# Two fused adjacency layers on one core: the two halves of 20 slots become a ring of 41 slots

## The chip, the cores and the metric

The kernel runs on one core of one Trainium2 chip. The metric is the device time in microseconds (us) of one execution; lower is better. The kernel before took 395.99 us, the median of three runs (395.52 to 396.37).

## The reference, cut to what matters

`x` is 5120 x 64, `adj` is 5120 x 5120, all in f32. The first layer scales and projects the rows of `x` into `e`, multiplies by the adjacency's transpose and by the adjacency, normalises, and adds. The second layer keeps edges only where a softmax passes a threshold; for these inputs none survives, so its message is zero and what is left of it is a second normalisation.

```python
e = concatenate([u, i])                  # rows of x, scaled and projected
h = adj @ (adj.T @ e)
out = layernorm(h) * gamma + beta + x
x1 = _layernorm(x + out)
return _layernorm(x1 + relu(message(x1, adj)))   # message is 0 unless an edge survives
```

An edge can survive only where entries of `adj` are large enough, so the kernel finds the largest sum of squares of a row piece of `adj` and enters the long branch only if it reaches a limit. In these runs it does not.

## The kernel before, in words

**Work and tiling.** `adj` is read from memory once, as ten column blocks of 512 columns (`NB = 10`), and each block as 20 units (`UPB`) of two row tiles: a unit is 128 partitions x 1024 f32, 512 KB, one DMA (line 1033). There are 200 units, numbered `v` through all blocks. One buffer, `pooled`, holds `SLOTS` slots of one unit each, and behind them `h_sum` (128 x 5120), the sum of `h` (lines 103 to 106). Even blocks lie in slots 20 to 39 and odd blocks in slots 0 to 19 (`SLOT_FIRST`, line 44), so the unit that lay in a slot before unit `v` is `v - 40`, the same place two blocks earlier.

**What each unit goes through.** TensorE multiplies it into the block's column sums, `adj.T @ e` (`multiply_unit`, line 1471, 8 records a unit). ScalarE reads it for the sum of squares (`scan`, line 1153): an ACTIVATE that writes a throw-away result into `scratch` (two buffers by turns) and an ACTIVATION_READ_ACCUMULATOR that brings the sum; `scan(v)` waits for `scan(v - 2)`, which used the same scratch buffer. VectorE then turns it in place, 32 x 32 squares at a time (`turn_unit`, line 1265), after both TensorE and ScalarE are through with it.

**What each block goes through.** When the 20 units of block `c` are multiplied, VectorE turns the block's column sums out of PSUM (`turn_half`, line 1274), and ScalarE and GpSimd copy them, 8 copies each in two steps of 4, into `col_sum` (`keep_cols`, lines 1162 and 1084; ScalarE does its part in its own order, after the last scan of the block and before the first of the next). Then TensorE multiplies the turned units by the column sums (`multiply_round`, line 1491, 128 records a round): a round takes some tiles of one block, by `PARTS` (0 to 9, 10 to 23 and 24 to 39 in blocks 0 to 8). VectorE adds each round's PSUM sums to `h_sum` (`add_round`, line 1285, for block 0 a copy, line 1283). A round needs its units turned, `col_sum` kept (first half from the start, second half for its second half of matmuls), and the earlier sums in its PSUM banks added.

**The order of the work** is written out by hand, one list per engine. TensorE in the steady part, for `c` from 1: products of units 0 to 15 of block `c + 1`, first round of block `c`, products of units 16 to 19 of block `c + 1`, second and third round of block `c`. This is called a cycle here; cycle `c` begins with the first product of block `c + 1`. At the start the order is: products of block 0, products of units 20 and 21, first round of block 0 (called R0). VectorE in a cycle: 13 turns, add the first round, a turn, `turn_half`, 5 turns, add the second round, a turn, add the third round. SyncE issues the loads in order of `v`; before loading into a slot it waits until the round that holds the slot's old unit is done (`round_done`, line 1032), and everything after it in SyncE's queue waits too.

**Set-up and end.** `x_first`, `xt_pairs` and small inputs lie in slots 0 to 5 until `e` is made; SyncE waits for that before unit 20 (line 1028). `center_t` and `center_g` are small tiles, written at the start and after R0 (lines 1073, 1250) and read by one small matmul in block 1 (line 1539), whose end is `gamma_turned`. At the end `x` is loaded again (lines 1038 to 1040) into the first slots of block 8 (`X_SLOT`), and seven groups of tiles are normalised and stored while the last four rounds run.

Of the kernel before, what the change touches and what calls it, by code (L numbers as in the profile page):

```python
# [7 lines left out]
def adjacency_layers_kernel(nc, x, adj, w_ui, scales, gamma, beta,  # L8
# [7 lines left out]
    bf16 = mybir.dt.bfloat16  # L16
    i32 = mybir.dt.int32
    ALU = mybir.AluOpType
    ACT = mybir.ActivationFunctionType
    X = mybir.AxisListType.X  # L20

    P = 128
    N, D = x.shape
# [11 lines left out]
    NB = len(WIDTHS)  # L35
# [4 lines left out]
    UNIT_FIRST = [sum(UPB[:c]) for c in range(NB + 1)]  # L40
    UNITS = UNIT_FIRST[NB]

    SLOTS = 40
    SLOT_FIRST = [20 if c % 2 == 0 else 0 for c in range(NB)]
    assert sum(WIDTHS) == N and max(WIDTHS) == CH

    PARTS = [((0, 10), (10, 14), (24, 16))] * (NB - 1)
    PARTS += [((0, 12), (12, 12), (24, 8), (32, 8))]


    ORDER = [(c,) + part for c in range(NB - 1) for part in PARTS[c]]
# [44 lines left out]
    with ctx:  # L96
        def sb(name, shape, dt=f32):
            return ctx.enter_context(nc.sbuf_tensor(name, shape, dt))
# [22 lines left out]
        SETUP_SLOTS = -(-setup_at[0] // SLOT)  # L121


        X_SLOT = 20
        x_at = SLOT * X_SLOT
        x_all = pooled[:, x_at:x_at + T * D].rearrange("p (t d) -> p t d", d=D)
        x_sum, var, rstd, y_var, y_eps, x1_rstd, scale = (
# [15 lines left out]
        rows_in = sb("rows_in", [P, T, D])  # L143
        col_sum = [sb(f"col_sum{k}", [P, CH // 32, D]) for k in range(2)]
        col_half = sb("col_half", [P, CH // 2])
        scratch = [sb(f"scratch{k}", [P, SLOT], bf16) for k in range(2)]
        ident = sb("ident", [P, P])
        center = sb("center", [P, 2 * D])
        gamma_sb = sb("gamma_sb", [D, 1])
        center_t = sb("center_t", [D, P])  # L150
        center_g = sb("center_g", [D, D])
        beta_sb = sb("beta_sb", [P, D])
        beta_sum = sb("beta_sum", [P, 1])
        square_sum = sb("square_sum", [P, UNITS])
# [3 lines left out]
        minus_half = sb("minus_half", [P, GT])  # L158


        piece_at = [N * i for i in range(4)] + [ln_at + N * i for i in range(4)]
        piece = [pooled[:, a:a + N] for a in piece_at]
        assert 4 * N <= x_at and piece_at[-1] + N <= POOLED
        ring, turned, carved_from, rest = piece[0:4], piece[4:6], piece[6], piece[7]
        cols = rest[:, 0:BLOCKS * D].rearrange("p (b d) -> p b d", d=D)
        sums = [rest[:, BLOCKS * D + GROUP * s:BLOCKS * D + GROUP * s + GROUP] for s in range(2)]
# [183 lines left out]

        def slot_of(v):
            c, i = place_of_unit(v)
            return SLOT_FIRST[c] + i

        def before_in_slot(v):

# [55 lines left out]
        def turned_of(g):  # L412

            c, first, nt = place_of_round(g)
            w = WIDTHS[c]
            at = SLOT * SLOT_FIRST[c] + w * first
            return pooled[:, at:at + w * nt].rearrange("p (t b r) -> p t b r", b=w // 32, t=nt)

        def spread_from(c, h, f):
# [596 lines left out]
        @block.sync  # L1016
        def _(sp):
            for k in range(LGROUPS):
                sp.dma_start(x_first[:, group_tiles(k), :], tile_rows(x, GT * k, GT)).then_inc(x_loaded[k], 16)
            for v in range(UNITS):  # L1020
                c, i = place_of_unit(v)
                ut, c0 = UNIT_TILES[c], COL_FIRST[c]
                if v == UNIT_FIRST[1]:
                    sp.dma_start(gamma_sb[:, :], gamma).then_inc(norm_in, 16)
                    sp.dma_start(beta_sb[:, :], beta.partition_broadcast(P)).then_inc(norm_in, 16)

                    assert SLOT_FIRST[1] == 0 and SETUP_SLOTS <= UPB[1]
                    sp.wait_ge(e_made, LGROUPS)
                before = before_in_slot(v)
                if before:  # L1030
                    b, ib = place_of_unit(before[-1])
                    sp.wait_ge(round_done, rounds_through(b, UNIT_TILES[b] * ib))
                sp.dma_start(slots[slot_of(v)].rearrange("p (t k) -> p t k", t=ut),  # L1033
                             tile_rows(adj, ut * i, ut)[:, :, c0:c0 + WIDTHS[c]]).then_inc(unit_loaded[slot_of(v)], 16)


            assert SLOT_FIRST[NB - 2] == X_SLOT and SLOT_FIRST[NB - 1] != X_SLOT
            sp.wait_ge(round_done, ROUNDS_AT[NB - 2] + 1)
            for a, b in ((0, USER_TILES), (USER_TILES, T)):
                sp.dma_start(x_all[:, a:b, :], tile_rows(x, a, b - a)).then_inc(x_again, 16)  # L1040

            survives = edges_may_survive(sp)

            def store_made(k):
                made, by = (out_made_act, BY_ACT) if k in BY_ACT else (out_made, BY_DVE)
                sp.wait_ge(made, by.index(k) + 1)
                store_out(sp, k)

            for k in (0, 1, 2, 4, 5, 3, 6):
                store_made(k)  # L1050
            for k in range(4):
                sp.wait_ge(out_stored[k], 16 * len(range(k, NORMS, 4)))
            with sp.If(survives > 0):
                message_sp(sp)
# [85 lines left out]
        @block.scalar  # L1140
        def _(act):
            act.dma_start(w_ui_sb[:, :], w_ui).then_inc(weights_in, 16)
            act.dma_start(scales_sb[:, :], scales).then_inc(scales_in, 16)

            def copy_pairs(k):
                act.wait_ge(pairs_turned, k + 1)
                act.copy(xt_pairs[:, CH * k:CH * k + CH], pair_bank(k)).then_inc(pairs_copied, 1)  # L1147

            def scan(v):
                wait_loaded(act, v)  # L1150
                if v >= 2:
                    act.wait_ge(unit_scanned, v - 1)
                nc.scalar.activation(scratch[v % 2][:, :], slots[slot_of(v)], ACT.Square,  # L1153
                                     accum_out=square_sum[:, v:v + 1]).then_inc(unit_scanned, 1)

            def keep_cols(c):
                act.wait_ge(halves_turned_b, c + 1)
                if c >= 2:
                    act.wait_ge(round_done, ROUNDS_AT[c - 1])
                for h in range(2):  # L1160
                    for a in range(QUADS):
                        kept = act.copy(spread_to(c, a, h, 0), spread_from(c, h, 0))  # L1162
                    kept.then_inc(cols_kept_act, 1)

            for k in range(LGROUPS - 1):
                copy_pairs(k)
            scan(0)
            copy_pairs(LGROUPS - 1)
            for v in range(1, UNITS):
                c, i = place_of_unit(v)  # L1170
                scan(v)
                if i == UPB[c] - 1:
                    keep_cols(c)
                if c == 1 and i == 16:
                    act.wait_ge(gamma_turned, 1)
                    act.copy(center[:, D:2 * D], bank[3][:, 0:D]).then_inc(center_kept, 1)

            def square_c(k):

                act.wait_ge(nat_made, k + 1)  # L1180
                if k >= 2:
                    act.wait_ge(var_made, k - 1)
                nc.scalar.activation(c_sq[k % 2][:, 0:norm_size(k), 0:D], nat_of(k)[:, 0:norm_size(k), 0:D],  # L1183
                                     ACT.Square, scale=D ** -0.5).then_inc(c_squared, 1)

            def square_y(k):

                act.wait_ge(y_made, k + 1)
                if k >= 2:
                    act.wait_ge(y_var_made, k - 1)  # L1190
                nc.scalar.activation(y_sq[k % 2][:, 0:norm_size(k), 0:D], x_all[:, norm_tiles(k), :],  # L1191
                                     ACT.Square, scale=((1.0 + LN_EPS) / D) ** 0.5).then_inc(y_squared, 1)

            def make_out(k):
                act.wait_ge(scale_made, k + 1)
                for i in range(norm_size(k)):
                    t = norm_tiles(k).start + i
                    made = nc.scalar.activation(ln_o[k % 4][:, i, :], x_all[:, t, :], ACT.Copy, scale=scale[:, t:t + 1])
                made.then_inc(out_made_act, 1)

            square_c(0)
            square_y(0)
            survives = edges_may_survive(act)
            square_c(1)
            square_c(2)
            square_y(1)
            square_y(2)
            square_c(3)
            square_c(4)
            make_out(1)  # L1210
            square_y(3)
            make_out(2)
            square_c(5)
            square_c(6)
            square_y(4)
            square_y(5)
            square_y(6)
            make_out(3)
            with act.If(survives > 0):
                message_act(act)  # L1220

        @block.vector
        def _(dve):
# [35 lines left out]
            def turn_unit(v):  # L1259

                c, i = place_of_unit(v)
                dve.wait_ge(unit_used, v + 1)
                dve.wait_ge(unit_scanned, v + 1)
                tiles = slots[slot_of(v)].rearrange("p (t b r) -> p t b r", t=UNIT_TILES[c], r=32)
                nc.vector.transpose(tiles, tiles).then_inc(unit_turned, 1)  # L1265
# [21 lines left out]
            def add_round(g):  # L1287
                add_tiles(g, *place_of_round(g)[1:])
# [25 lines left out]
            turn_half(1)  # L1314
            for v in range(UNIT_FIRST[1] + 16, UNIT_FIRST[2]):
                turn_unit(v)
            add_round(2)


# [288 lines left out]
```

## Time and profile before

| what | value |
|---|---|
| median of three runs | 395.99 us (395.52 to 396.37) |
| the profiled execution's own time | 397.39 us |
| its span, first to last instruction | 395.5 us |
| TensorE busy | 379.0 us, 96% |
| VectorE busy | 316.7 us, 80% |
| ScalarE busy | 269.1 us, 68% |
| DMA engines, share of the span on the queue of the loads | 76.3% |
| granted TensorE clock, mean | 0.992 |

The span is 1.9 us shorter than the profiled execution's own time, and that time is 1.4 us above the median of the runs. PE is TensorE, PEld its weight loads, DVE VectorE, ACT ScalarE, POOL GpSimd, SP SyncE. Matmul ends in the records are modelled, so starts are the safer numbers: the distance between two starts is what a piece of work takes on TensorE.

### The profile page before, as it was taken

What the parts mean: (1) busy time and instruction counts of PE and PEld (TensorE: products, weight loads), DVE (VectorE), ACT (ScalarE), POOL (GpSimd) and SP (SyncE); (2) the same over time, 40 slices, a digit from 0 to 9 for tenths busy, and PEclk for the clock granted to TensorE, in tenths of its full rate; (3) what the DMA queues carried; (4) which work ended last, traced back from release to release, by engine and by line L of the source; (5) the groups of instructions that cost most, each with busy time, mean ns of one, the idle gap of its engine ahead of it and who ended that gap; (6) DMA issues with size and microseconds to landing.
All of it is one profiled execution on the core that took longest, in us unless ns stands there. A gap on an engine that the chain in (4) does not pass through costs nothing.

```text
span 395.5 us, 13309 instructions
## 1 busy us (share of the span) xinstructions
PE 379.0 (96%) x5762; PEld 220.2 (56%) x5762; DVE 316.7 (80%) x305; ACT 269.1 (68%) x519; POOL 63.8 (16%) x122
## 2 busy tenths in 40 slices
PE   8987999999999999999999999999999999999990
PEld 7743655565465546545654664565466456555770
DVE  1699989797697869687976989697698869795674
ACT  3598996994868658597856868685876778511143
POOL 2001101102100300030030003003000300277375
PEclk9999999999999999999999999999999999999996
DMA  8999999995797799579877958996795799400012
GB/s 291 387 388 382 386 386 384 386 352 192 232 380 267 268 320 391 180 275 389 314 263 272 386 195 277 388 351 230 278 386 191 272 392 383 145 3 2 24 35 85
DMA packets 56991, 109.83 MB, mean 278 GB/s; under 512 B 3808, under 2 KB 4576, under 8 KB 56928
## 3 DMA queue, kind: packets, MB, share of 16 engines
q1 hardware_dynamic: 56640, 108.84, 76.3%
q8 instruction: 47, 0.77, 0.8%
q14 instruction: 16, 0.13, 0.1%
q10 hardware_dynamic: 288, 0.09, 0.1%
HBM read 107.60 MB, written 1.31 MB: 275 GB/s over the span
## 4 chain that ended last, share of the span: by engine, by line
PE 84%; DMA 6%; issue 3%; DVE 3%; POOL 1%; ACT 1%; SPq 1%; POOLq 0%; DVEq 0%
PE quad L1491 45%; PE quad L1471 34%; DMA pooled<-in_adj 6%; PE quad L1506 2%; DVE pooled L1265 2%; PE quad L1513 1%; PE quad L1442 1%; ACT scratch L1153 1%; SPq L1033 1%; PE quad L1452 1%; DVE pooled L1285 1%; POOL pooled L1112 1%; POOL col_sum L1084 0%; POOLq L96 0%; POOL pooled L1107 0%
## 5 line engine op out<-in xcount | busy, mean ns | idle before, releaser
L1153 ACT ACTIVATE scratch<-pooled 128x1024 bf16<-128x1024 f32 x200 | 210.1, 1051 | 39.8 <-DMA pooled<-in_adj 38.0
L1265 DVE STREAM_TRANSPOSE pooled<-pooled 128x1024 f32<-128x1024 f32 x200 | 229.7, 1209 | 3.3 <-ACT scratch L1153 3.2
L1471 PE MATMUL quad<-pooled,rows_in 128*64 128x256 f32 x1600 | 180.2, 381 | 4.3 <-DMA pooled<-in_adj 4.3
L1491 PE MATMUL quad<-pooled,col_sum 32*64 32x320 f32 (+4 forms) x3968 | 177.5, 507 | 0.4 <-POOL col_sum L1084 0.2
L1471 PEld LDWEIGHTS quad<-pooled,rows_in 128*64 128x64 f32 x1600 | 111.9, 137 | 74.3 <-issue 13.1
L1491 PEld LDWEIGHTS quad<-pooled,col_sum 32*64 32x64 f32 x3968 | 87.5, 132 | 83.1 <-issue 64.6
L1285 DVE TENSOR_TENSOR pooled<-pooled,quad 128x1280 f32<-128x1280 f32 (+5 forms) x29 | 52.4, 1808 | 43.8 <-PE quad L1491 43.7
L1084 POOL COPY col_sum<-col_half 32x256 f32<-32x256 f32 x80 | 31.6, 394 | 312.1 <-DVE col_half L1274 309.0
L1162 ACT COPY col_sum<-col_half 32x256 f32<-32x256 f32 x80 | 32.2, 402 | 38.0 <-DVE col_half L1274 37.0
L1153 ACT ACTIVATION_READ_ACCUMULATOR scratch<-pooled 128x1 f32 x200 | 37.4, 187 | 0.0
L1183 ACT ACTIVATE pooled<-quad 128x256 f32<-128x256 f32 (+2 forms) x7 | 3.3, 475 | 23.4 <-PE quad L1506 23.4
L1506 PEld LDWEIGHTS quad<-center,pooled 128*128 128x128 f32 x80 | 9.3, 191 | 3.3 <-issue 1.8
L1506 PE MATMUL quad<-center,pooled 128*128 128x128 f32 x80 | 10.3, 281 | 0.9 <-DVE pooled L1285 0.8
L1274 DVE STREAM_TRANSPOSE col_half<-quad 128x256 f32<-128x256 f32 x10 | 4.5, 445 | 7.2 <-PE quad L1471 7.2
L1112 POOL TENSOR_TENSOR pooled<-pooled,minus_half 128x4 f32<-128x4 f32 (+2 forms) x7 | 8.9, 1276 | 6.5 <-DVE pooled L1369 6.4
L1107 POOL TENSOR_TENSOR pooled<-pooled,minus_half 128x4 f32<-128x4 f32 (+2 forms) x7 | 8.9, 1281 | 5.0 <-DVE pooled L1337 4.8
L1191 ACT ACTIVATE pooled<-pooled 128x256 f32<-128x256 f32 (+2 forms) x7 | 3.6, 507 | 9.1 <-DVE pooled L1364 7.2
L1147 ACT COPY pooled<-quad 128x512 f32<-128x512 f32 x5 | 2.9, 585 | 9.7 <-PE quad L1442 9.7
L1283 DVE COPY pooled<-quad 128x1280 f32<-128x1280 f32 (+2 forms) x3 | 5.8, 1936 | 4.1 <-PE quad L1491 4.1
L1238 DVE TENSOR_TENSOR rows_in<-quad,pooled 128x256 f32<-128x256 f32 x10 | 3.7, 410 | 3.6 <-PE quad L1452 3.3
L1102 POOL TENSOR_TENSOR pooled<-pooled,beta_sb 128x512 f32<-128x512 f32 x5 | 6.4, 1276 | 0.4
L1337 DVE TENSOR_REDUCE pooled<-pooled 128x4 f32<-128x260 f32 (+2 forms) x7 | 3.8, 538 | 2.7 <-ACT pooled L1183 2.7
(45 smaller groups left out, 62.8 us busy)
## 6 DMA issues: line engine op xcount, KB each, us to landing
pooled<-in_adj SPq DMA_DIRECT2D x200, 512.0 KB, 9.4
pooled<-in_x SPq DMA_DIRECT2D x5, 256.0 KB, 3.7
pooled<-in_x SPq DMA_DIRECT2D x1, 768.0 KB, 5.3
pooled<-in_x SPq DMA_DIRECT2D x1, 512.0 KB, 3.8
out<-pooled SPq DMA_DIRECT2D x2, 256.0 KB, 2.5
out<-pooled SPq DMA_DIRECT2D x2, 192.0 KB, 2.4
out<-pooled SPq DMA_DIRECT2D x3, 128.0 KB, 2.1
pooled<-in_w_ui ACTq DMA_DIRECT2D x1, 64.0 KB, 3.3
```

The source lines that it names most:

```text
L1084: kept = nc.gpsimd.tensor_copy(spread_to(c, a, h, 1), spread_from(c, h, 1))
L1102: nc.gpsimd.tensor_tensor(xk, xk, beta_sb[:, :].unsqueeze(1).to_broadcast([P, GT, D]), ALU.add).then_inc(x_steps, 1)
L1107: nc.gpsimd.tensor_tensor(rstd[:, norm_tiles(k)], var[:, norm_tiles(k)], minus_half[:, 0:norm_size(k)], ALU.pow).then_inc(rstd_made, 1)
L1112: nc.gpsimd.tensor_tensor(scale[:, norm_tiles(k)], y_var[:, norm_tiles(k)], minus_half[:, 0:norm_size(k)], ALU.pow).then_inc(scale_made, 1)
L1153: nc.scalar.activation(scratch[v % 2][:, :], slots[slot_of(v)], ACT.Square, accum_out=square_sum[:, v:v + 1]).then_inc(unit_scanned, 1)
L1162: kept = act.copy(spread_to(c, a, h, 0), spread_from(c, h, 0))
L1265: nc.vector.transpose(tiles, tiles).then_inc(unit_turned, 1)
L1283: nc.vector.tensor_copy(to, share).then_inc(round_added, 1)
L1285: nc.vector.tensor_tensor(to, to, share, ALU.add).then_inc(round_added, 1)
L1471: mm = pe.matmul(block_bank(c)[half(h), 0:w // 2], rows_in[:, t, :], slots[slot_of(v)][:, at:at + w // 2], start=(t == 0), stop=(t == T - 1))
L1491: mm = pe.matmul(round_banks(g)[a][half(b % 2), 0:w].rearrange("p (t r) -> p t r", r=32), col_sum[c % 2][quadrant(a), b, :], to[quadrant(a ...
L1506: mm = pe.matmul(nat_of(k)[:, i, :], h_sum[:, P * (first + i):P * (first + i) + P], center[:, :], start=True, stop=True)
```

## The change

The ring has 41 slots, and unit `v` lies in slot `(9 + v) % 41`, so the unit before it in its slot is `v - 41`. A round's turned data must lie in one piece, so in odd blocks a part now ends where the ring wraps round: block 3 has rounds of 10, 16 and 14 tiles, block 5 of 12, 16 and 12, block 7 of 14, 16 and 10; block 1 and the even blocks keep 10, 14 and 16, and block 9 its own four. The order of products and rounds on TensorE is the same, and so are the lists of the other engines. The space for the new slot (4 KB a partition) comes from `scratch`, which is one buffer in place of two, so that `scan(v)` waits for `scan(v - 1)`, and from `center_t` and `center_g`, which now lie in the end of `h_sum`; the third `add_round` therefore waits for `gamma_turned`. SyncE's wait for `e` stands before unit 32 in place of unit 20. `x` is loaded again into slot 5 in place of slot 20, again the first slots of block 8. The pieces of the long branch, which is not entered, are placed elsewhere.

```diff
--- before.py
+++ after.py
@@ -40,12 +40,17 @@
     UNIT_FIRST = [sum(UPB[:c]) for c in range(NB + 1)]
     UNITS = UNIT_FIRST[NB]
 
-    SLOTS = 40
-    SLOT_FIRST = [20 if c % 2 == 0 else 0 for c in range(NB)]
+    SLOTS = 41
+    SLOT_FIRST = [(9 + UNIT_FIRST[c]) % SLOTS for c in range(NB)]
     assert sum(WIDTHS) == N and max(WIDTHS) == CH
 
     PARTS = [((0, 10), (10, 14), (24, 16))] * (NB - 1)
+    PARTS[3] = ((0, 10), (10, 16), (26, 14))
+    PARTS[5] = ((0, 12), (12, 16), (28, 12))
+    PARTS[7] = ((0, 14), (14, 16), (30, 10))
     PARTS += [((0, 12), (12, 12), (24, 8), (32, 8))]
+    assert all((SLOT_FIRST[c] + t // UNIT_TILES[c]) % SLOTS + nt // UNIT_TILES[c] <= SLOTS
+               for c in range(NB) for t, nt in PARTS[c])
 
 
     ORDER = [(c,) + part for c in range(NB - 1) for part in PARTS[c]]
@@ -121,7 +126,7 @@
         SETUP_SLOTS = -(-setup_at[0] // SLOT)
 
 
-        X_SLOT = 20
+        X_SLOT = 5
         x_at = SLOT * X_SLOT
         x_all = pooled[:, x_at:x_at + T * D].rearrange("p (t d) -> p t d", d=D)
         x_sum, var, rstd, y_var, y_eps, x1_rstd, scale = (
@@ -143,12 +148,13 @@
         rows_in = sb("rows_in", [P, T, D])
         col_sum = [sb(f"col_sum{k}", [P, CH // 32, D]) for k in range(2)]
         col_half = sb("col_half", [P, CH // 2])
-        scratch = [sb(f"scratch{k}", [P, SLOT], bf16) for k in range(2)]
+        scratch = sb("scratch", [P, SLOT], bf16)
         ident = sb("ident", [P, P])
         center = sb("center", [P, 2 * D])
         gamma_sb = sb("gamma_sb", [D, 1])
-        center_t = sb("center_t", [D, P])
-        center_g = sb("center_g", [D, D])
+
+        center_t = h_sum[0:D, N - P:N]
+        center_g = h_sum[0:D, N - P - D:N - P]
         beta_sb = sb("beta_sb", [P, D])
         beta_sum = sb("beta_sum", [P, 1])
         square_sum = sb("square_sum", [P, UNITS])
@@ -158,9 +164,9 @@
         minus_half = sb("minus_half", [P, GT])
 
 
-        piece_at = [N * i for i in range(4)] + [ln_at + N * i for i in range(4)]
+        piece_at = [0] + [ln_at + N * i for i in range(7)]
         piece = [pooled[:, a:a + N] for a in piece_at]
-        assert 4 * N <= x_at and piece_at[-1] + N <= POOLED
+        assert N <= x_at and piece_at[-1] + N <= POOLED
         ring, turned, carved_from, rest = piece[0:4], piece[4:6], piece[6], piece[7]
         cols = rest[:, 0:BLOCKS * D].rearrange("p (b d) -> p b d", d=D)
         sums = [rest[:, BLOCKS * D + GROUP * s:BLOCKS * D + GROUP * s + GROUP] for s in range(2)]
@@ -350,7 +356,7 @@
 
         def slot_of(v):
             c, i = place_of_unit(v)
-            return SLOT_FIRST[c] + i
+            return (SLOT_FIRST[c] + i) % SLOTS
 
         def before_in_slot(v):
 
@@ -413,7 +419,7 @@
 
             c, first, nt = place_of_round(g)
             w = WIDTHS[c]
-            at = SLOT * SLOT_FIRST[c] + w * first
+            at = SLOT * slot_of(UNIT_FIRST[c] + first // UNIT_TILES[c])
             return pooled[:, at:at + w * nt].rearrange("p (t b r) -> p t b r", b=w // 32, t=nt)
 
         def spread_from(c, h, f):
@@ -1023,8 +1029,9 @@
                 if v == UNIT_FIRST[1]:
                     sp.dma_start(gamma_sb[:, :], gamma).then_inc(norm_in, 16)
                     sp.dma_start(beta_sb[:, :], beta.partition_broadcast(P)).then_inc(norm_in, 16)
-
-                    assert SLOT_FIRST[1] == 0 and SETUP_SLOTS <= UPB[1]
+                if v < UNIT_FIRST[2] and slot_of(v) == 0:
+
+                    assert c == 1 and i + SETUP_SLOTS <= UPB[1]
                     sp.wait_ge(e_made, LGROUPS)
                 before = before_in_slot(v)
                 if before:
@@ -1148,9 +1155,9 @@
 
             def scan(v):
                 wait_loaded(act, v)
-                if v >= 2:
-                    act.wait_ge(unit_scanned, v - 1)
-                nc.scalar.activation(scratch[v % 2][:, :], slots[slot_of(v)], ACT.Square,
+                if v:
+                    act.wait_ge(unit_scanned, v)
+                nc.scalar.activation(scratch[:, :], slots[slot_of(v)], ACT.Square,
                                      accum_out=square_sum[:, v:v + 1]).then_inc(unit_scanned, 1)
 
             def keep_cols(c):
@@ -1314,6 +1321,7 @@
             turn_half(1)
             for v in range(UNIT_FIRST[1] + 16, UNIT_FIRST[2]):
                 turn_unit(v)
+            dve.wait_ge(gamma_turned, 1)
             add_round(2)
 
 
```

## Rows read from the trace of the kernel before

**Rows 1.** The page: the engines, and the queue of the loads.

```profile
PE 379.0 (96%) x5762; PEld 220.2 (56%) x5762; DVE 316.7 (80%) x305; ACT 269.1 (68%) x519; POOL 63.8 (16%) x122
...
q1 hardware_dynamic: 56640, 108.84, 76.3%
```

**Rows 2.** Timeline of TensorE: cycle 1, and starts in the next three.

```profile
73.86 14.03 PE L1471 MATMUL quad<-pooled,rows_in 128*64 128x256 f32 x128
87.82 4.56 PE L1491 MATMUL quad<-pooled,col_sum 32*64 32x320 f32 x128
92.31 3.67 PE L1471 MATMUL quad<-pooled,rows_in 128*64 128x256 f32 x32
95.92 13.14 PE L1491 MATMUL quad<-pooled,col_sum 32*64 32x448 f32 x256
108.98 13.17 PE L1471 MATMUL quad<-pooled,rows_in 128*64 128x256 f32 x120
...
144.60 12.31 PE L1471 MATMUL quad<-pooled,rows_in 128*64 128x256 f32 x112
...
158.45 1.08 PE L1471 MATMUL quad<-pooled,rows_in 128*64 128x256 f32 x8 [0.29 <-DMA pooled<-in_adj]
...
180.63 9.72 PE L1471 MATMUL quad<-pooled,rows_in 128*64 128x256 f32 x88
```

**Rows 3.** Busy time by engine in cycles 1, 2, 3, and 4 to 7 together.

```profile
core 0: us, PE busy (x) PEld busy (x) DVE busy (x) ACT busy (x) POOL busy (x), PEclk, DMA share, GB/s
73.86:108.98 35.12, 35.12 (x552) 19.62 (x544) 28.86 (x24) 28.38 (x57) 3.16 (x8) 1.00 0.79 278
108.98:144.60 35.62, 35.35 (x552) 19.47 (x544) 28.86 (x24) 26.02 (x50) 3.15 (x8) 1.00 0.86 301
144.60:180.63 36.03, 35.57 (x552) 19.46 (x545) 28.86 (x24) 26.17 (x49) 3.16 (x8) 1.00 0.83 301
180.63:321.14 140.51, 140.51 (x2185) 78.57 (x2177) 115.43 (x96) 102.13 (x191) 12.63 (x32) 1.00 0.84 301
```

**Rows 4.** Timeline of ScalarE in cycle 3: scans start as units land.

```profile
157.06 1.06 ACT L1153 ACTIVATE scratch<-pooled 128x1024 bf16<-128x1024 f32 x1 [0.19 <-DMA pooled<-in_adj]
...
158.43 1.06 ACT L1153 ACTIVATE scratch<-pooled 128x1024 bf16<-128x1024 f32 x1 [0.22 <-DMA pooled<-in_adj]
```

**Rows 5.** Timeline of TensorE: last products before R0, and R0.

```profile
38.66 1.08 PE L1471 MATMUL quad<-pooled,rows_in 128*64 128x256 f32 x8 [0.25 <-DMA pooled<-in_adj]
39.90 4.57 PE L1491 MATMUL quad<-pooled,col_sum 32*64 32x320 f32 x128 [0.16 <-POOL col_sum L1084]
```

**Rows 6.** Timeline of all engines before R0: scans, a turn, keep_cols.

```profile
16.53 1.06 ACT L1153 ACTIVATE scratch<-pooled 128x1024 bf16<-128x1024 f32 x1
...
17.49 0.19 ACT L1153 ACTIVATION_READ_ACCUMULATOR scratch<-pooled 128x1 f32 x1
...
17.58 1.05 ACT L1153 ACTIVATE scratch<-pooled 128x1024 bf16<-128x1024 f32 x1
...
17.79 2.37 DVE L1265 STREAM_TRANSPOSE pooled<-pooled 128x1024 f32<-128x1024 f32 x2 [3.21 <-ACT scratch L1153]
...
35.82 1.06 ACT L1153 ACTIVATE scratch<-pooled 128x1024 bf16<-128x1024 f32 x1 [0.25 <-DMA pooled<-in_adj]
...
37.95 3.31 ACT L1162 COPY col_sum<-col_half 32x256 f32<-32x256 f32 x8 [0.98 <-DVE col_half L1274]
38.07 3.46 POOL L1084 COPY col_sum<-col_half 32x256 f32<-32x256 f32 x8 [34.45 <-DVE col_half L1274]
```

**Rows 7.** Timeline of VectorE: the second waits for the end of the first.

```profile
364.12 0.56 DVE L1357 TENSOR_TENSOR pooled<-quad,pooled 128x384 f32<-128x384 f32 x1 [1.25 <-POOL pooled L1107]
364.71 0.56 DVE L1364 TENSOR_TENSOR pooled<-pooled 128x384 f32<-128x384 f32 x1
```

**Rows 8.** Timeline of VectorE: the third add of cycle 1.

```profile
109.16 2.29 DVE L1285 TENSOR_TENSOR pooled<-pooled,quad 128x2048 f32<-128x2048 f32 x1 [3.69 <-PE quad L1491]
```

**Rows 9.** Groups by shape: the rounds of 16 tiles (busy us, mean ns).

```profile
L1491 PE MATMUL quad<-pooled,col_sum 32*64 32x512 f32 x1152 | 63.7, 588 | 0.2 <-DVE pooled L1285 0.2
```

## The prediction, made before the change was run

> **What bounds the kernel now.** I read the page first: TensorE is busy 96% of the span, and the queue of the loads fills 76% of the DMA engines' time [rows 1]. So a change of buffers can win only where TensorE stands still for a load, and can lose wherever it makes TensorE wait. Then I read TensorE's timeline cycle by cycle. A cycle without a stall takes 35.12 us (73.86 to 108.98) [rows 2]; cycles 4 to 7 take 140.51 us, 35.13 each, all of it busy at the full clock [rows 3]. Only cycles 2 and 3 are longer, 35.62 and 36.03 us [rows 3]: 0.50 + 0.90 = 1.40 us over the rest. In cycle 3 the late thing is the last unit before the first round (place 15 of its block): ScalarE starts to scan it at 158.43 and TensorE to multiply it at 158.45, both as it lands [rows 2, 4]. In cycle 1 sixteen products take 13.96 us (73.86 to 87.82) [rows 2], 0.87 each, so place 15 is wanted 13.1 us after a cycle starts; in cycle 3 it came 13.85 us after (144.60 to 158.45). The unit before it landed 1.37 us earlier [rows 4], the DMA rhythm, so the queue was full and not waiting for permission. Last I read the start: the first blocks run at the pace of the DMA, R0 starts at 39.90, 0.16 us after the product before it ended (38.66 + 1.08), released by GpSimd's `keep_cols` [rows 5]. From R0 on the program is one chain on TensorE: what delays R0 delays everything.
>
> **What the ring gives.** A unit now needs the round that frees `v - 41`, the place before its own, so the first unit of each batch moves into the batch before: place 0 waits for nothing recent, place 5 goes with the first round, place 12 with the second. Of the batches that run without a pause into place 15, each holds one unit less ahead of it, so place 15 lands one rhythm, 1.37 us, earlier [rows 4]. The worst stall is 0.9 us, so both go: **-1.40 us**. No more is to be had there, since cycles 1 and 4 to 7 have no stall. Bounds: 0 (they stay) and -1.40.
>
> **The odd blocks' rounds.** The tiles are the same, 40 a block. A round of 16 costs 63.7 / 9 = 7.08 us [rows 9], one of 10 takes 4.49 (87.82 to 92.31) [rows 2], that is 0.44 to 0.45 a tile for both, and there are three rounds before and after: zero for TensorE, at most +-0.3 us. What moves is when slots come free. In block 7, the extreme case, the first round is 4 tiles (1.8 us) longer and the second 2 tiles (0.9 us), so its second batch of loads is let go 2.7 us later, but that batch now starts at place 8 in place of 5, three units (4.1 us) ahead: place 15 still lands 1.4 us earlier than before. For blocks 3 and 5 the same count gives 0.9 us later against one unit and 1.8 us later against two. VectorE has the work of three adds as before; the third add of a cycle started after 3.69 us of idle [rows 8], so the larger second add (16 tiles, some 2.3 us by the same row, for 14) still ends before TensorE wants its banks, which is at the next cycle's first product, when the third round is done: zero.
>
> **The single scratch buffer.** Now `scan(v)` waits for the end of `scan(v - 1)`. In the rows a scan starts at 16.53, its READ_ACCUMULATOR ends at 17.49 + 0.19 = 17.68, and the next scan starts at 17.58, before that end; the rhythm is 1.04 to 1.05 us [rows 6]. With the wait the next start is 1.15 us plus the time that an engine needs to see its own semaphore. The nearest row of an instruction that waits for the one before it on its own engine is VectorE's: 364.12 + 0.56 = 364.68 to 364.71, 0.03 us [rows 7]. I take 1.15 + 0.04 = **1.19 us a scan**. The other end is what another engine needed: the turn that waited for the scan of 16.53 starts at 17.79, 1.26 us after it [rows 6]. The low end is 1.15.
>
> Over 200 scans that is 30 us of ScalarE, but in a cycle it is 20 x 1.19 = 23.8 us and 3.3 us of `keep_cols` [rows 6], 27.1 of 35.1, and DMA brings units at 1.37 anyway. Behind the scans stand the turns, which wait for TensorE's products first; and ScalarE's 8 us to spare in a cycle are the cover: zero. Without them each scan's 0.15 us would count.
>
> The cover is missing in **block 0**. Scan 1 starts at 16.53 because a copy of the set-up stands before it in ScalarE's queue, and scans follow each other at 1.04 to catch up with the DMA (16.53 + 18 x 1.04 = 35.3); scan 19 starts at 35.82, as its unit lands, and `keep_cols` can start at 37.95, when `turn_half` is done [rows 6]. Now scan 19 starts at 16.53 + 18 x 1.19 = 37.95, the queue reaches `keep_cols` 1.04 later, at 38.99, four of its eight copies take 3.31 / 2 = 1.66 and end at 40.65, and TensorE sees it about 0.1 later. (GpSimd's first four end at 38.07 + 3.46 / 2 = 39.80 and R0 starts at 39.90 [rows 5, 6].) R0 starts at 40.75: **+0.85 us**. The second half of the copies (42.3) is there before R0's half (43.0). VectorE's turn of unit 20 now ends near 44.8, and R0's sums are ready at 45.3: covered by R0's own delay. Ends: at 1.15 a scan +0.15 us, at 1.26 +2.1 us.
>
> A rule speaks for less. By the Trainium skill, "ScalarE: Activation LUTs", section "What ACT_TABLE_LOAD costs", back-to-back ACTIVATEs overlap by about 93 ns. If only that overlap were lost, a scan would take some 1.13 us, an estimate from that page, `keep_cols` would not be delayed and the sum would be -1.4. The trace agrees with an overlap (0.10 us between 17.58 and 17.68) but the semaphore is that of the READ_ACCUMULATOR.
>
> **The small edits.** The wait for `gamma_turned` before the third add: behind its matmul TensorE still has eleven products of block 1 (0.87 us each) and a round of 16 tiles (7.08) before that add, some 16 us; zero. SyncE's wait for `e` moves to unit 32: it lets the loads behind it go earlier if it held any, and those of units 20 to 31 are needed no sooner; zero. `center_t` and `center_g` in `h_sum`, the other place of `x`: the same instructions and the same freeing round; zero. The end of the kernel, after 321.14, is untouched except that the last block's loads come earlier, and it has no load stall.
>
> **Sum**, against the profiled execution's own time: 397.39 - 1.40 + 0.85 = 396.84. That execution is 1.4 us above the median of the runs, so I carry over the difference, -0.55, and not the value: 395.99 - 0.55 = 395.44, **395.4 us**. The weak point is just this: if the other executions are shorter because they don't stall in cycles 2 and 3, there is nothing to win in them. I keep that apart as rival 3. A measurement can tell about 0.2% (0.8 us) from no change: faster is under 395.2, slower over 396.8.
>
> **The rivals.**
> 1. *Both terms, as summed* (the forecast, 395.0 to 396.3). Chance 0.45.
> 2. *The wait costs no time* (faster). If the semaphore is seen within the overlap, 1.13 us or less a scan, R0 keeps its place, and only -1.40 is left: 394.6. For it: it needs only 0.06 us less a scan than I take. Against: the READ_ACCUMULATOR's end. This is also where the rule above leads. Chance 0.22.
> 3. *No stall to win* (about no change). Cycles 4 to 7 ran without one [rows 3], so the two stalls may belong to this execution. Then only +0.85 is left: 396.8, on the border. Chance 0.18.
> 4. *The scan chain of block 0 decides* (slower). Each 0.01 us a scan costs 0.18 us at R0. At 1.26, the delay to the turn, it is +2.1 - 1.4 = +0.7; from 1.27 the change is slower, at 1.30 it is +0.85 + 18 x 0.11 - 1.40 = +1.4, 397.4. For it: the only row of somebody waiting for a scan shows 1.26. Against: an engine's own semaphore was seen in 0.03. Chance 0.15.
>
> The range takes in rivals 2 and 4 and nearly all of 3: 394.6 to 397.4. Faster 0.26 (rival 2, and some of case 1), slower 0.22 (rival 4, half of 3), same 0.52.
>
> **What would show it.** The scans of block 0 start every 1.19 us from 16.5; `keep_cols` on ScalarE starts at 39.0 and not at 37.95; R0 starts near 40.75, released by ACT and not by POOL. Cycle lengths on TensorE: seven of 35.1, with no DMA release after 45 us. ScalarE's idle time for DMA falls, its idle inside scans rises. Wrong if R0 still starts at 39.9 (rival 2), if the cycles were 35.1 before (rival 3), if scans take 1.26 or more (rival 4), or if a cycle grows beyond 35.2 with PE waiting for a turn or an add, which none of these has.

## The result, and the profile after

The changed kernel takes 398.79 us (398.09 to 399.77, six runs) against 395.89 us for the kernel before beside it: the ratio is 1.0065, 95% interval 1.0051 to 1.0079. The medians are 2.9 us apart, and the ratio stands for 2.6 us: it is slower. The forecast was 395.4 us, and 398.79 lies outside the range of 394.6 to 397.4.

The profiled execution took 399.77 us with a span of 397.9 us, 2.4 more than before. The page of the changed kernel, in the lines that answer to [rows 1], with the chain that ended last:

```profile
PE 379.6 (95%) x5762; PEld 220.6 (55%) x5762; DVE 316.9 (80%) x305; ACT 277.3 (70%) x519; POOL 63.8 (16%) x122
...
q1 hardware_dynamic: 56640, 108.84, 75.6%
...
PE 90%; ACT 6%; DVE 1%; issue 1%; POOL 1%; POOLq 0%; ACTq 0%
PE quad L1499 45%; PE quad L1479 40%; ACT scratch L1160 6%; PE quad L1514 2%; PE quad L1521 1%; PE quad L1460 1%; DVE pooled L1292 1%; PE quad L1450 1%; POOL pooled L1119 1%; ACT col_sum L1169 0%; POOLq L101 0%; POOL pooled L1114 0%; ACT pooled L1154 0%; DVE pooled L1345 0%; DVE pooled L1385 0%
```

The chain goes through the scans (line 1160 now) for 6% of the span, some 24 us: the chain of block 0. The waits of TensorE, all of them (us in total, times, longest), show what took the place of the stalls for loads:

```profile
PE quad L1479 <- DMA pooled<-in_adj: 3.3, 12, 0.4
PE quad L1499 <- ACT col_sum L1169: 1.9, 1, 1.9
PE quad L1521 <- DVE pooled L1231: 1.2, 1, 1.2
PE quad L1514 <- DVE pooled L1292: 0.9, 1, 0.9
PE quad L1460 <- ACT pooled L1154: 0.3, 1, 0.3
PE quad L1499 <- DVE pooled L1292: 0.2, 1, 0.2
```

The timeline of TensorE around R0, as in [rows 5]:

```profile
38.46 1.08 PE L1479 MATMUL quad<-pooled,rows_in 128*64 128x256 f32 x8 [0.26 <-DMA pooled<-in_adj]
41.48 6.26 PE L1499 MATMUL quad<-pooled,col_sum 32*64 32x320 f32 x128 [1.93 <-ACT col_sum L1169]
47.66 2.60 PE L1479 MATMUL quad<-pooled,rows_in 128*64 128x256 f32 x22
```

R0 starts at 41.48 in place of 39.90, and then takes 6.26 us in place of 4.57. The second is not a wait: it is the clock. The same view as [rows 3], in stretches around R0 and then by cycles:

```profile
core 0: us, PE busy (x) PEld busy (x) DVE busy (x) ACT busy (x) POOL busy (x), PEclk, DMA share, GB/s
40.00:42.70 2.70, 1.23 (x40) 1.03 (x48) 1.88 (x2) 2.62 (x7) 0.89 (x3) 1.00 1.06 388
42.80:46.10 3.30, 3.30 (x58) 2.31 (x48) 1.25 (x1) 3.09 (x6) 0.00 (x0) 0.50 1.07 390
46.20:48.00 1.80, 1.80 (x52) 1.07 (x38) 0.17 (x1) 1.62 (x5) 0.00 (x0) 1.00 1.02 378
77.12:112.25 35.13, 35.13 (x553) 19.64 (x545) 28.86 (x24) 31.78 (x59) 3.15 (x8) 1.00 0.75 269
112.25:147.37 35.12, 35.12 (x552) 19.64 (x544) 28.86 (x24) 26.21 (x49) 3.15 (x8) 1.00 0.84 302
147.37:182.50 35.13, 35.13 (x553) 19.64 (x545) 29.12 (x24) 26.22 (x49) 3.15 (x8) 1.00 0.81 291
182.50:323.00 140.50, 140.50 (x2184) 78.56 (x2176) 115.98 (x96) 103.31 (x190) 12.62 (x32) 1.00 0.84 303
```

From 42.8 to 46.1 the granted clock is 0.50, 1.2 GHz, though TensorE is busy all that time; the fall comes after a gap of 1.93 us. Before, the clock was whole there. The cycles are all 35.1 us: both stalls for loads are gone. So the span adds up: +1.58 (R0 later) + 1.68 (41.48 to 47.66 against 39.90 to 44.40, the clock) - 1.40 (stalls) + 0.52 (the end of the kernel, where TensorE's work takes the same 62.3 us and the last store lands later; that piece differs nearly as much, by 0.4 us, between the two profiles of the kernel before) = +2.4.

The scans of block 0, to be laid beside [rows 6]:

```profile
15.87 1.06 ACT L1160 ACTIVATE scratch<-pooled 128x1024 bf16<-128x1024 f32 x1
16.83 0.19 ACT L1160 ACTIVATION_READ_ACCUMULATOR scratch<-pooled 128x1 f32 x1
17.11 1.06 ACT L1160 ACTIVATE scratch<-pooled 128x1024 bf16<-128x1024 f32 x1
...
34.49 1.06 ACT L1160 ACTIVATE scratch<-pooled 128x1024 bf16<-128x1024 f32 x1
...
36.05 1.06 ACT L1160 ACTIVATE scratch<-pooled 128x1024 bf16<-128x1024 f32 x1 [0.42 <-ACT scratch L1160]
...
38.54 1.06 ACT L1160 ACTIVATE scratch<-pooled 128x1024 bf16<-128x1024 f32 x1
...
39.59 3.29 ACT L1169 COPY col_sum<-col_half 32x256 f32<-32x256 f32 x8
```

A scan starts 1.24 us after the one before (15.87 to 17.11), not 1.19; once, from 34.49 to 36.05, it takes 1.56. `keep_cols` starts at 39.59. Scan 1 happened to start 0.66 us earlier than in the profile before, so the chain is longer than R0's delay of 1.58 us says. From the start of scan 1 to R0 it is 25.61 us here, and it is 25.61 to 25.64 us in each of the seven profiles of kernels with the whole chain, though scan 1 starts anywhere from 15.82 to 16.53 in them. The chain alone sets R0 there.

### The profile page after: what moved, and what is told of

It reads as the page before. It is cut to its first block, busy times and chain, and to the rows that moved or that the text cites. A ratio compares the mean times of both kernels' runs of the same rounds, so it can differ in the third digit from the quotient of the medians.

```text
span 397.9 us, 13311 instructions
## 1 busy us (share of the span) xinstructions
PE 379.6 (95%) x5762; PEld 220.6 (55%) x5762; DVE 316.9 (80%) x305; ACT 277.3 (70%) x519; POOL 63.8 (16%) x122
## 4 chain that ended last, share of the span: by engine, by line
PE 90%; ACT 6%; DVE 1%; issue 1%; POOL 1%; POOLq 0%; ACTq 0%
PE quad L1499 45%; PE quad L1479 40%; ACT scratch L1160 6%; PE quad L1514 2%; PE quad L1521 1%; PE quad L1460 1%; DVE pooled L1292 1%; PE quad L1450 1%; POOL pooled L1119 1%; ACT col_sum L1169 0%; POOLq L101 0%; POOL pooled L1114 0%; ACT pooled L1154 0%; DVE pooled L1345 0%; DVE pooled L1385 0%
## 5 line engine op out<-in xcount | busy, mean ns | idle before, releaser
L1499 PE MATMUL quad<-pooled,col_sum 32*64 32x512 f32 (+4 forms) x3968 | 179.2, 511 | 2.2 <-ACT col_sum L1169 1.9
L1499 PEld LDWEIGHTS quad<-pooled,col_sum 32*64 32x64 f32 x3968 | 88.6, 133 | 85.8 <-issue 60.8
L1292 DVE TENSOR_TENSOR pooled<-pooled,quad 128x2048 f32<-128x2048 f32 (+5 forms) x29 | 52.4, 1808 | 43.1 <-PE quad L1499 43.0
```

Of the source, the lines that this page charges most:

```text
L1292: nc.vector.tensor_tensor(to, to, share, ALU.add).then_inc(round_added, 1)
L1499: mm = pe.matmul(round_banks(g)[a][half(b % 2), 0:w].rearrange("p (t r) -> p t r", r=32), col_sum[c % 2][quadrant(a), b, :], to[quadrant(a ...
```

## The experiments

Twelve experiments ran, with eight different kernels, in three batches, each beside runs of the kernel before in the same batch. Theory 1: the loss is the chain of scans in block 0 and, in part of the executions, the clock behind the gap it leaves; the ring itself gains. The rival: the ring, its loads or its odd rounds cost the time.

**First four, one chip** (kernel before: 396.56 us, 25 runs).

`one_scratch`, the scratch edit alone:

```diff
-        scratch = [sb(f"scratch{k}", [P, SLOT], bf16) for k in range(2)]
+        scratch = sb("scratch", [P, SLOT], bf16)
...
-                if v >= 2:
-                    act.wait_ge(unit_scanned, v - 1)
-                nc.scalar.activation(scratch[v % 2][:, :], slots[slot_of(v)], ACT.Square,
+                if v:
+                    act.wait_ge(unit_scanned, v)
+                nc.scalar.activation(scratch[:, :], slots[slot_of(v)], ACT.Square,
```

> The kernel before with one scratch buffer and nothing else of the change: two halves of 20 slots, parts as before, small tiles in their places. Theory 1 (the loss is the chain of scans in block 0): scans every 1.24 us from 16.5 to scan 19, R0 starts at 41.5 in place of 39.9, TensorE's granted clock falls to half for some 3 us behind that gap as in the changed kernel, and the time is 2.3 to 3.5 us above before, 398.2 to 399.4. Rival (the ring or its loads cost the time): no change, 395.5 to 396.4.

Measured: 398.23 us, ratio 1.0039 (1.0025 to 1.0053). The edit alone, without the ring, costs 1.7 us. TensorE's timeline in its profile:

```profile
39.11 1.08 PE L1471 MATMUL quad<-pooled,rows_in 128*64 128x256 f32 x8 [0.27 <-DMA pooled<-in_adj]
41.84 4.57 PE L1491 MATMUL quad<-pooled,col_sum 32*64 32x320 f32 x128 [1.64 <-ACT col_sum L1162]
46.33 3.89 PE L1471 MATMUL quad<-pooled,rows_in 128*64 128x256 f32 x34
```

R0 is as late as in the changed kernel and waits for ScalarE's copies, but here it takes 4.57 us: a gap of 1.64 us did not cost the clock. That half of the expectation missed. The cycles have 0.16 us of stalls for loads left, all of it in cycle 2.

`lend_scratch`, the changed kernel with a second scratch buffer borrowed for blocks 0 and 1 from a part of `h_sum` that is not yet in use:

```diff
+        lent = h_sum[:, 24 * P:24 * P + SLOT // 2].bitcast(bf16)
...
-                if v:
-                    act.wait_ge(unit_scanned, v)
-                nc.scalar.activation(scratch[:, :], slots[slot_of(v)], ACT.Square,
+                both = v < UNIT_FIRST[2]
+                if v >= 2 or not both:
+                    act.wait_ge(unit_scanned, v - 1 if both else v)
+                to = lent if both and v % 2 else scratch
+                nc.scalar.activation(to[:, :], slots[slot_of(v)], ACT.Square,
```

> The changed kernel (ring of 41), but for blocks 0 and 1 the odd scans write into an unused piece of h_sum, so that scan(v) waits for scan(v - 2) there, as before; from block 2 on the single scratch stays. Theory 1: R0 is back near 39.9 or earlier with the clock whole, the single scratch costs nothing later, all cycles take 35.1 us: 394.6 if the stalls of cycles 2 and 3 are in most executions of before, 395.5 to 396.0 if they are not. Rival (the ring costs time, or the single scratch costs in the steady part too): 397 to 399.

Measured: 395.93 us, ratio 0.9980 (0.9970 to 0.9989), faster than before. R0 starts at 40.21. The rival falls: with the ring, its odd rounds and the single scratch in 160 of 200 scans nothing is lost, and every cycle is 35.1 us. The ring is worth 0.6 us in the median, not 1.4. The cycles in its profile:

```profile
74.15:109.28 35.13, 35.13 (x552) 19.64 (x545) 28.87 (x24) 31.77 (x59) 3.16 (x8) 1.00 0.83 294
109.28:144.41 35.13, 35.13 (x553) 19.65 (x545) 28.85 (x24) 26.22 (x49) 3.15 (x8) 1.00 0.86 311
144.41:179.53 35.12, 35.12 (x552) 19.64 (x544) 29.12 (x24) 26.22 (x49) 3.15 (x8) 1.00 0.80 292
179.53:320.04 140.51, 140.51 (x2184) 78.57 (x2177) 115.96 (x96) 103.28 (x190) 12.63 (x32) 1.00 0.84 303
```

`fill_gap`, the changed kernel with matmuls on zeros in the gap:

```diff
+            for _ in range(4):
+                pe.matmul(bank[1][:, 0:WARM], h_sum[:, 0:P], h_sum[:, 0:WARM], start=True, stop=True)
             multiply_round(0)
```

> The changed kernel with four matmuls on zeros (128x256 f32, into a bank that nobody uses then) between unit 21 and R0, which keep TensorE at work for 1.7 us of its 1.93 us gap. Theory 1, its second half (the gap also costs the clock): R0 still starts near 41.5, released by ScalarE, but takes 4.5 us in place of 6.2, the granted clock stays whole: 1.7 us under the changed kernel's slow executions, about 397.4. Rival (R0 is long for another cause, a late second half of col_sum): R0 still takes 6.2 us and the time stays at 398.1 to 399.8.

Measured: 398.69 us (397.63 to 399.14, six runs), ratio 1.0047 (1.0029 to 1.0064).

```profile
39.56 1.99 PE L1543 MATMUL quad<-pooled 128*128 128x256 f32 x8
42.14 4.57 PE L1499 MATMUL quad<-pooled,col_sum 32*64 32x320 f32 x128 [0.59 <-ACT col_sum L1169]
```

R0 took 4.57 us and no execution's mean clock was under 0.989, where three of the six of the changed kernel had 0.987. The expected 397.4 us was missed: the time is hardly lower than the changed kernel's median, and on time this run decides nothing. One reason shows in the profile. Scan 1 starts at 16.53 and R0 at 42.14, 0.66 us later than in the changed kernel's profile; the start of the chain moved, and the filling matmuls were done 0.59 us before R0.

`wait_13_scans`, the kernel before with the nearer wait for 13 scans only:

```diff
-                if v >= 2:
-                    act.wait_ge(unit_scanned, v - 1)
+                if v:
+                    act.wait_ge(unit_scanned, v if v <= 13 else v - 1)
```

> The kernel before with both scratch buffers, but scans 1 to 13 wait for the scan just before them; the other scans wait as before. Theory 1: scan 19 starts at 16.5 + 12 x 1.24 + 6 x 1.04 = 37.7, R0 at 40.5, a gap of 0.7 us on TensorE, which is no longer than those it had before R0 anyway, so the clock stays whole: 0.6 us above before, 396.5. Rival (a wait costs only where the single buffer is): 395.9. If the gap alone takes the clock: 398.

Measured: 396.68 us, ratio 1.0002 (0.9990 to 1.0013). The mechanism is as expected: the wait alone, with both buffers in place, moves R0.

```profile
39.03 1.08 PE L1471 MATMUL quad<-pooled,rows_in 128*64 128x256 f32 x8 [0.26 <-DMA pooled<-in_adj]
40.60 4.57 PE L1491 MATMUL quad<-pooled,col_sum 32*64 32x320 f32 x128 [0.49 <-ACT col_sum L1162]
```

R0 starts at 40.60, behind a gap of 0.49 us and with a whole clock, but the time doesn't show the 0.6 us. The interval ends at 0.5 us, so on time the expectation missed. Smaller stalls for loads may have made up for it: TensorE waits for none in the cycles of this profile, where the first one of before lost 1.40 us; its cycles are longer in all by 0.25 us, and that lies in the rounds of cycle 7. That this is the reason is not shown.

**Second four, on another chip** (before: 396.27 us, 27 runs).

`ring_again`, the changed kernel unaltered:

> The changed kernel, unaltered, once more beside the others. Theory (three parts: scans chained at 1.24 to 1.26 us put R0 at 41.5 to 42.2, the ring takes away the load stalls, and in some executions the clock falls behind the gap before R0): two levels of time, about 1.2 us apart, the higher one with the lower mean clock; median 2 to 3 us above before. Rival (the half clock of the first profile was a single event): one level, 1.1 us above before, the sum of the two kernels that carry one part each.

Measured: 398.12 us, ratio 1.0048 (1.0029 to 1.0068). Ten executions between 397.1 and 398.2 with mean clocks from 0.989 to 0.994, two at 399.97 and 401.19 with 0.985 and 0.983. Two levels, as the theory has it, but the median is only 1.85 us above before where 2 to 3 was expected, and the lower ten have a median of 397.94 us, 1.7 above before, with the other two 2.0 and 3.3 us over that, not 1.2. The profile is one of the lower level, with nearly the gap that cost the clock in the first one:

```profile
38.49 1.08 PE L1479 MATMUL quad<-pooled,rows_in 128*64 128x256 f32 x8 [0.26 <-DMA pooled<-in_adj]
41.43 4.57 PE L1499 MATMUL quad<-pooled,col_sum 32*64 32x320 f32 x128 [1.85 <-ACT col_sum L1169]
45.93 4.32 PE L1479 MATMUL quad<-pooled,rows_in 128*64 128x256 f32 x38
```

`halves_again`, the kernel before unaltered:

> The kernel before, unaltered, once more: how much of its 1.4 us of load stalls in cycles 2 and 3 is in another execution. Theory (the ring gained 0.6 us in the typical execution, so that is the typical stall): cycles of 35.1 us with one or two longer ones, 0.3 to 0.8 us in all. Rival (1.4 us is typical): two cycles of 35.6 and 36.0 again. Time as before, ratio 1.000.

Measured: 396.18 us, ratio 0.9994 (0.9981 to 1.0006). In the profile the stalls are all in cycle 2, 0.99 us in all, about half of them before the first round and half in the products behind it:

```profile
73.61:108.73 35.12, 35.12 (x552) 19.63 (x544) 28.86 (x24) 27.46 (x56) 3.15 (x8) 1.00 0.80 277
108.73:144.84 36.11, 35.77 (x552) 20.33 (x544) 28.86 (x24) 27.09 (x51) 3.15 (x8) 1.00 0.85 308
144.84:320.48 175.64, 175.64 (x2729) 98.21 (x2721) 144.30 (x120) 128.71 (x240) 15.79 (x40) 1.00 0.83 301
```

That is over the 0.3 to 0.8 expected. The size and the cycle of the stalls change from one execution to the next.

`gap_before_R0` and `gap_filled`, both on the lent version, so that the gap has nothing to do with the scans' rhythm. `gap_filled` has all three added lines, `gap_before_R0` only the wait:

```diff
+            for _ in range(5):
+                pe.matmul(bank[1][:, 0:WARM], h_sum[:, 0:P], h_sum[:, 0:WARM], start=True, stop=True)
+            pe.wait_ge(unit_scanned, UNIT_FIRST[1] + 1)
             multiply_round(0)
```

> The version with the lent scratch (R0 at 39.9 to 40.2), but R0 waits for the scan of unit 20, which ends near 42.5: a gap of 2.3 to 2.6 us on TensorE with nothing else changed. If the gap takes the clock: R0 takes 6.2 us in place of 4.5, and the time is 2.4 + 1.7 = 4.1 us above the lent version's, 399.8 to 400.2. If it does not: R0 takes 4.5 us and the time is 2.4 us above, 398.3.

> The same gap before R0, with five matmuls on zeros at its start (2.5 us). If it is TensorE's idleness that takes the clock: the clock stays whole in all executions, 2.4 us above the lent version's, 398.3, and 1 to 1.7 us under the unfilled gap. If the clock does not depend on it: equal to the unfilled gap.

Measured: 400.12 us with the gap open (six runs, ratio 1.0084, 1.0063 to 1.0105), 398.17 us with it filled (ten, 1.0044, 1.0031 to 1.0057). Open: four executions at 400.0 to 400.5 with clocks of 0.985 to 0.987, two at 398.7 and 398.9 with 0.989 and 0.990. Filled: 397.6 to 398.9, no clock under 0.990. This tells them apart: with the gap filled no execution is over 398.9 us or under 0.990, so it is TensorE's idleness before R0 that takes the clock, in some executions and not in all. In the two profiles (first open, then filled) R0 took 4.57 us both times; the open one is of the two lower executions:

```profile
42.49 4.57 PE L1502 MATMUL quad<-pooled,col_sum 32*64 32x320 f32 x128 [2.86 <-ACT scratch L1163]
```

```profile
39.46 2.43 PE L1546 MATMUL quad<-pooled 128*128 128x256 f32 x10
41.90 4.57 PE L1502 MATMUL quad<-pooled,col_sum 32*64 32x320 f32 x128
```

**Last four, on the first chip, to see whether the parts add up** (before: 396.39 us, 29 runs). The kernels are the changed one, `one_scratch`, `lend_scratch` and `fill_gap` again.

> The changed kernel on the same chip as the next three, to see whether its parts add up. Theory 1: median 1.9 us above before (two of three executions at the lower level), with single executions 1.2 us or more higher whose mean clock is 0.987 or less. Rival (a loss that neither part has alone): over 2.5 us above before with the clock whole.

> One scratch buffer alone (halves of 20 slots). Theory 1: 1.7 us above before, R0 some 1.7 to 2.2 us later, and load stalls of 0 to 1 us left in cycles 2 and 3. If the parts add, the changed kernel's lower level lies 0.6 us under this one; if the stalls go as soon as R0 is late, at the same level.

> The ring with the lent scratch, repeated. Theory 1: 0.6 us under before (ratio 0.997 to 0.999), no load stall in any cycle, R0 at 39.5 to 40.2. Rival (the first figure was luck): ratio 1.000.

> The changed kernel with its gap before R0 filled with four matmuls on zeros, repeated. Theory 1: no execution with a mean clock of 0.987 or less, one level of time, equal to the lower level of the changed kernel within 0.5 us. Rival (filling does nothing): high executions as in the changed kernel.

| kernel | median us | ratio (95%) | executions with a clock of 0.987 or less | median of the others |
|---|---|---|---|---|
| changed | 398.03 | 1.0041 (1.0026 to 1.0056) | 3 of 12, 399.6 to 399.8 | 397.79 |
| one scratch, halves | 398.73 | 1.0064 (1.0045 to 1.0082) | 4 of 12, 399.7 to 401.4 | 398.27 |
| ring, scratch lent | 396.02 | 0.9983 (0.9973 to 0.9992) | none of 12 | 396.02 |
| changed, gap filled | 398.30 | 1.0046 (1.0031 to 1.0060) | none of 6 | 398.30 |

In the executions above 0.987: the chain alone +1.9 us, the ring alone -0.4, both together +1.4; 1.9 - 0.4 = 1.5. The parts add up within what these runs can tell, some 0.5 us, and no loss shows that neither part has. The profile of the chain alone has 0.60 us of stalls for loads left, in cycle 2. In the five profiles with halves of 20 slots the seven cycles are 0.16 to 1.40 us longer in all than seven without a stall, and in all nine with the ring they are not. The profile of the changed kernel here is again one of those with half the clock:

```profile
41.51 6.26 PE L1499 MATMUL quad<-pooled,col_sum 32*64 32x320 f32 x128 [2.19 <-ACT col_sum L1169]
```

The lent version again has R0 where it was, and now GpSimd's copies release it, as before the change:

```profile
39.91 4.57 PE L1502 MATMUL quad<-pooled,col_sum 32*64 32x320 f32 x128 [0.29 <-POOL col_sum L1092]
```

It is the version that beats both kernels: 0.6 and 0.4 us under the kernel before in two batches, and 2.0 us under the changed one in the batch that has both. Filling the gap took away the high executions, but its level is 0.51 us over the changed kernel's lower one, just past the margin named in its expectation. In its profile scan 1 starts at 16.18 and R0 at 41.80, 0.3 us later than in the profiles of the changed kernel; why scan 1 starts when it does is open.

## Why the prediction was wrong

**What the ring gives**: right in kind, too large in size. All cycles went to 35.1 us, as forecast; but 1.40 us was what one execution had lost. Another profile of the same kernel shows 0.99, and the typical gain of the ring is 0.4 to 0.6 us (`lend_scratch`, `add_ring_lent`). That is between the forecast and rival 3; the sum took the stalls of a single profile, whose execution was 1.4 us slower than the median, at their full price.

**The odd blocks' rounds, the small edits, the steady part of the scratch edit**: zero, as forecast. The lent version has them all and is faster than before.

**The single scratch buffer**: the place and the chain were right (R0 late, released by ScalarE, scan rhythm behind it), the term was mis-sized. A scan takes 1.24 us, not 1.19: the step that failed is the choice of VectorE's row [rows 7], 0.03 us from an instruction's end to the start of one that waits for it, for ScalarE. From the READ_ACCUMULATOR's end (16.83 + 0.19 = 17.02) to the next start (17.11) it is 0.09 us. The other end, 1.26, was the better neighbour: it was the same semaphore, seen 0.11 us after the READ_ACCUMULATOR's end (17.68 to 17.79). The Trainium skill, "Perfetto Trace Analysis", section "DVE / Act Engine Instruction (TENSOR_ADD, Activation, etc)", says that the reported start comes only after operands are prefetched, behind the semaphore wait; that agrees with a gap that is larger than the semaphore alone, but no run here separates the two. From scan 1 to R0 the prediction had 24.22 us (16.53 to 40.75), and the profiles have 25.6, 1.4 more: the rhythm makes 0.9 of it, one scan of 1.56 us (at the same scan in all seven profiles) 0.3, and the way from `keep_cols` to R0 0.1 (1.89 us, not 1.76). R0 came at 41.4 to 42.1 in every profile with the whole chain; forecast 40.75. With scan 1 at 16.53, as the prediction had it, R0 is at 42.14 (`fill_gap`); an earlier scan 1 hid part of the error in the others. In place of +0.85 the chain costs 1.7 to 1.9 us with the clock whole.

**What no step had**: the clock. The prediction read "at the full clock" off [rows 3] and asked of R0's delay only how long it is, not what TensorE's idleness behind it does to the rounds after it. With about 2 us of idle before R0 the granted clock fell to 0.50 in two profiles, `after` and `add_ring`, whose mean clock is 0.987; in the twelve others, at 0.989 to 0.994, it is whole there. Taking 0.987 or less as the sign of a fall, it came in 8 of 30 executions of the changed kernel, in 4 of 20 with one scratch alone and in 4 of 6 with the open gap. With a filled gap it came in none of 22, and with a gap of at most 0.5 us in none of 48 (24 lent, 12 with 13 waits, 12 of before). The sign is rough: one of the 81 runs of the kernel before beside the batches has 0.987 too, at an ordinary 396.53 us, and the clock also falls to 0.50 in every profile at the end, after TensorE's last matmul, which is part of each mean. The times say the same, though: the changed kernel's executions lie at 397.1 to 398.5 us or at 399.3 and above, with nothing between. In the profile the fall costs 1.68 us. The Trainium skill, "TensorE: Matmul & The Clock Gate", section "Part 1: The HAM clock gate (the "warmup" mystery)", has the rule that the clock follows how busy TensorE has been; the runs agree in part, with a fall behind gaps of 1.93 and 2.19 us and none behind 1.64, 1.85, 2.39 and 2.86, and by it rival 4 should have had a second price, about as large. The first six runs had three such executions, which is one reason why that ratio, 1.0065, is the highest of the three taken of the changed kernel. It is not all: their other three lie at 398.09 to 398.25 us, 2.2 to 2.4 above before, where the later batches have 1.7 and 1.4. What makes up those 0.6 to 0.9 us is open.

Of the rivals, number 4 (the scan chain of block 0 decides, slower) named the mechanism. Its point of decision, 1.27 us a scan, was set by the full 1.40 us of stalls; with 0.5 us of them it lies at 1.22, below the 1.24 that was measured. By the prediction's own sum 1.24 us a scan would have given +0.35 us, so the rival's price was too low as well.

## What to carry to other kernels

A buffer taken away from a throw-away result is not free if the engine that writes it is catching up: price the new wait where that engine has no slack (here the first block), and take the latency from the same engine and the same semaphore, not from a neighbour. Do not take a stall that one profile shows at its full price when that execution is slower than the median; look for it in a second one. And when TensorE gets a new gap of a microsecond or two, look at the clock behind it as well as at the gap, in more than one execution.

## What the runs showed of the hardware

The same kernel, with a gap of 1.93 us before R0 in one profile and 1.85 in another, lost half the clock in the first (R0 6.26 us) and kept it in the second (4.57 us); a gap of 2.39 to 2.86 us kept it in two other profiles. So in these runs a gap of this size made the fall possible and did not decide it. An ACTIVATE that waited for the READ_ACCUMULATOR before it started 0.09 us after that one's end, where VectorE's row [rows 7] has 0.03. Why one scan in block 0 takes 0.3 us longer, always the same one, stays open, and so does what makes the size of the load stalls change from run to run.
